# A hybrid transformer layer on one core: weights loaded behind the first stacks

## The reference

```
x = x + attn_a(layernorm(x))   # 32 heads of 8, window of 128 keys back, softmax, Wo
x = x + ffn(layernorm(x))      # 256 -> 1024 -> 256, relu, shared weights
x = x + attn_b(layernorm(x))   # rms norm, conv of 4 taps, delta-rule scan over time, gated MLP
x = x + ffn(layernorm(x))      # the same ffn again

def ffn(x1):
    w_up = ((q_up - 7.5) * repeat(s_up, 64, axis=1)).T          # q_* are int32 in 0..15
    y1 = x1 @ w_up + b_up + x1 @ w_up_lora_a @ w_up_lora_b       # rank 16
    x2 = relu(y1)
    w_down = ((q_dn - 7.5) * repeat(s_dn, 64, axis=1)).T
    return x2 @ w_down + b_down + x2 @ w_down_lora_a @ w_down_lora_b
```

## Time and profile before

| | us |
|---|---|
| median of 3 runs | 1243.53 (1241.19 to 1246.96) |
| the profiled execution | 1244.26 |
| its span in the profile | 1242.3 |
| busy: PE, PEld, DVE, ACT, POOL | 1037.7, 712.3, 917.8, 495.8, 179.0 |

### The profile page before, as it was taken

The page is one execution under the profiler, slowest core; times in us unless marked ns, Lnnn a source line. Parts: engine busy times, 40 slices in busy tenths (PEclk is TensorE's granted clock), DMA queues, the critical chain, the costliest instruction groups (busy, mean ns, idle before and its releaser), DMA issues.

```text
span 1242.3 us, 23054 instructions
## 1 busy us (share of the span) xinstructions
PE 1037.7 (84%) x9098; PEld 712.3 (57%) x9112; DVE 917.8 (74%) x2425; ACT 495.8 (40%) x1027; POOL 179.0 (14%) x267
## 2 busy tenths in 40 slices
PE   3589869967998999899988999899989978966467
PEld 2245635645556665666566755666566646744445
DVE  2733277898789778987898778977898678968911
ACT  2034254326443554326432644355443634541122
POOL 2200001040004000400040000300040004010400
PEclk9579879886999899989999999989998979997768
DMA  9813014302430133012410242014400200020000
GB/s 285 153 35 76 17 43 102 61 1 72 101 50 1 35 109 79 9 35 81 89 28 10 77 100 45 1 42 103 82 7 26 82 16 1 18 77 0 5 21 9
DMA packets 94123, 67.81 MB, mean 55 GB/s; under 512 B 47744, under 2 KB 86848, under 8 KB 94016
## 3 DMA queue, kind: packets, MB, share of 16 engines
q1 hardware_dynamic: 88544, 60.75, 20.9%
q10 hardware_dynamic: 4960, 5.54, 1.6%
q0 software_dynamic: 512, 0.05, 0.1%
HBM read 45.57 MB, written 20.32 MB: 53 GB/s over the span
## 4 chain that ended last, share of the span: by engine, by line
PE 47%; DVE 28%; ACT 9%; DMA 7%; SPq 4%; issue 3%; POOL 1%; ACTq 0%; DVEq 0%; POOLq 0%
PE bank L1612 6%; PE bank L1503 5%; PE bank L1757 5%; PE bank L1560 4%; PE bank L1684 4%; PE bank L1766 4%; PE bank L1592 4%; DMA q_l<-lane_q 4%; PE bank L1709 3%; DVE state L1235 3%; DVE lane_buf L1213 3%; PE bank L1555 3%; DVE state L1227 3%; DVE u_l L1222 2%; DVE mx L1023 2%
## 5 line engine op out<-in xcount | busy, mean ns | idle before, releaser
L715 ACT ACTIVATE probs<-bank 128x512 f32<-128x512 f32 x256 | 152.1, 597 | 187.4 <-PE bank L1597 187.3
L1612 PE MATMUL bank<-probs,v_ext 128*9 128x128 f32 x2048 | 164.9, 283 | 16.5 <-ACT probs L715 6.8
L1023 DVE TENSOR_REDUCE mx<-bank 128x2 f32<-128x320 f32 x256 | 120.9, 486 | 54.3 <-PE bank L1560 50.3
L341 POOL TENSOR_TENSOR lane_buf<-state,q_l 128x128 f32<-128x128 f32 x128 | 79.9, 654 | 339.7 <-DVEq L1242 339.7
L1757 PE MATMUL bank<-feat_c,wgu 128*128 128x256 f32 (+1 forms) x384 | 96.3, 402 | 23.6 <-DVE hid_c L1284 18.0
L1612 PEld LDWEIGHTS bank<-probs,v_ext 128*9 128x9 f32 x2048 | 91.3, 93 | 39.6 <-issue 18.0
L1592 PE MATMUL bank<-q_stack,k_stack 128*128 128x128 bf16 x1024 | 106.0, 229 | 2.7 <-DMA q_stack<-m_rows 2.7
L1555 PE MATMUL bank<-edge_mask,identb 128*128 128x128 bf16 x256 | 63.0, 246 | 52.6 <-DVE mx L1023 36.6
L1757 PEld LDWEIGHTS bank<-feat_c,wgu 128*128 128x128 f32 (+1 forms) x384 | 71.8, 192 | 44.1 <-DVE hid_c L1284 21.2
L1213 DVE TENSOR_TENSOR lane_buf<-state,til 128x128 f32<-128x128 f32 x256 | 84.5, 330 | 16.9 <-POOL lane_buf L602 10.2
L1560 PE MATMUL bank<-k_stack,q_stack 128*32 128x160 bf16 x2048 | 93.0, 265 | 0.0
(11 more groups left out here) (169 smaller groups left out, 1762.5 us busy)
## 6 DMA issues: line engine op xcount, KB each, us to landing
k_pieces<-conv SPq DMA_DIRECT2D x48, 128.0 KB, 2.3
k_stack<-k_pieces SPq DMA_DIRECT2D x32, 192.0 KB
k_stack<-k_pieces SPq DMA_DIRECT2D x32, 128.0 KB
k_l<-lane_k SPq DMA_DIRECT2D x8, 512.0 KB, 3.7
q_l<-lane_q SPq DMA_DIRECT2D x8, 512.0 KB, 5.7
q_pieces<-conv SPq DMA_DIRECT2D x24, 128.0 KB, 2.1
q_stack<-q_pieces SPq DMA_DIRECT2D x32, 96.0 KB
tok<-in_x SPq DMA_DIRECT2D x8, 256.0 KB, 3.2
```

What stands on the lines that cost most here:

```text
L715: act.activation(probs[:, u % 2], score_bank[u % 2][:], ACT.Exp, scale=float(DK) ** -0.5).then_inc(exp_done, 1)
L1023: dve.tensor_reduce(mx[:, g, 2 * v:2 * v + 2], bank[1 + u % 2][:].rearrange("p (h k) -> p h k", h=2)[:, :, 0:SPAN], AX.X, ALU.max).then_in ...
L1612: last = pe.matmul(bank[5][row:row + VE, col:col + W], v_ext[:, b, kb, h, :], probs[:, u % 2, (hp * 2 + kb) * W:(hp * 2 + kb + 1) * W], st ...
```

## The change

The launch, the data and what is computed stay the same. On each engine:

- SP: the nine weights, `wdown_b`, three constants (ones, head_sum, to_lanes, now part of `plain`), the residual's x and the quantised weights with their scales are issued behind the three first stacks and x of block 1. The low-rank factors, which ScalarE's queue had, come ahead of the pieces. Of the pieces SP writes the keys (`first_keys`).
- ScalarE issues two DMAs at the start instead of 12; computes rstd before the copies of the attention weights; issues the three DMAs of the query pieces; and copies the eight banks of low-rank products into `w_up` and `w_dn` (`lora_kept`). It waits for `weights_in` at the first relu of block 0 rather than ahead of the first maxima.
- VectorE clears `k_stack` first of all and sets up `k_stack` before `q_stack`. `up_weights` runs at the slot of step 20 (WEIGHTS_AT) of the first attention, its twin for `w_dn`, `down_weights`, and `delta_weights` behind `first_apply` of block 0. The dequantised values are written over the scales, then added to what ScalarE copied.
- GpSimd issues the six pad DMAs of the first three slots (`first_pads`), behind its 16 group rows.
- TensorE multiplies `ident` by `ident` 56 times (WARM) into a bank that the next turns overwrite; waits for `lora_kept` ahead of the maxima, and for weights where each is used first.

```diff
+WARM = 56
+WEIGHTS_AT = 20
...
@@ plain and consts
+            (ones[:], a["ones"]),
+            (head_sum[:], a["head_sum"]),
+            (to_lanes[:], a["to_lanes"]),
         ]
-        consts = [(ones[:], a["ones"]), (head_sum[:], a["head_sum"]),
-                  (to_lanes[:], a["to_lanes"]), (edge_mask_f, a["edge_mask"]),
-                  (tri_mask_f, a["tri_mask"]), (stack_cols[:], a["stack_cols"])]
+        consts = [(edge_mask_f, a["edge_mask"]), (tri_mask_f, a["tri_mask"]), (stack_cols[:], a["stack_cols"])]
...
@@ SP
+            def first_keys():
+                for p, cast in enumerate((piece1, piece2, piece3)):
+                    sp.wait_ge(cast, 2)
+                    for late in range(2):
+                        sp.dma_start(k_pieces[late, :, :, 2 - p, :, 1 - late].rearrange("h b p t -> p (h b) t"),
+                                     pieces[:, 1, p, :].rearrange("p (a t) -> p a t", t=W)).then_inc(pieces_out, 16)
+            def quantised():
+                sp.dma_start(q_up.rearrange("p (k n) -> p k n", k=KT),
                             a["q_up"].rearrange("(k p) n -> p k n", p=128)).then_inc(up_in, 16)
...
-            for dst, src in plain:
-                sp.dma_start(dst, src).then_inc(weights_in, 16)
-            for i, m in inner:
-                sp.dma_start(wdown_b[0:m, i, :], a["wdown_b"][128 * i:128 * i + m, :]).then_inc(weights_in, 16)
-            load_residual(0)
-            pieces_to_dram(0)
+            for dst, src in [(lora_a_up, a["lora_a_up"]), (lora_b_dn, a["lora_b_dn"]),
+                             (lora_b_up, a["lora_b_up"]), (lora_a_dn, a["lora_a_dn"])]:
+                sp.dma_start(dst, src).then_inc(lora_in, 16)
+            first_keys()
             sp.wait_ge(pieces_out, 144)
             sp.wait_ge(pad_out, 48)
             sp.wait_ge(stack_init, 2)
             for g in range(RING):
                 load_stacks(0, g)
-                load_pad(0, g)
-            sp.wait_ge(tok_next_ready, 1)
             load_x(1)
+            quantised()
+            load_residual(0)
+            for dst, src in plain:
+                sp.dma_start(dst, src).then_inc(weights_in, 16)
+            for i, m in inner:
+                sp.dma_start(wdown_b[0:m, i, :], a["wdown_b"][128 * i:128 * i + m, :]).then_inc(weights_in, 16)
@@ GpSimd
+            pool.wait_ge(stack_init, 2)
+            for r in range(RING):
+                load_pad(pool, 0, r, first_pads)
@@ ScalarE
             act.wait_ge(early_in, 16 * (len(early) + 2))
+            norm_next(0)
             for k in range(KT):
                 last = act.copy(wqkv_a[:, k, 0:2 * D].rearrange("p (a d h) -> p a d h", d=DK, h=HPH),
                                qk_staged[:, k].rearrange("p (a h d) -> p a d h", d=DK, h=HPH))
-            norm_next(0)
             turn_next(0)
...
+            act.wait_ge(piece3, 2)
+            for p in range(3):
+                act.dma_start(q_pieces[0, :, :, p].rearrange("h b p t -> p (h b) t"),
+                              pieces[:, 0, p, :].rearrange("p (a t) -> p a t", t=W)).then_inc(pieces_out, 16)
             values_out(0)
-            act.wait_ge(weights_in, 16 * (len(plain) + IT))
+            for k in range(KT):
+                for c in range(2):
+                    act.wait_ge(lora_prod, 2 * k + c + 1)
+                    act.copy(w_up[:, k, c * 512:(c + 1) * 512], bank[2 * k + c][:]).then_inc(lora_kept, 1)
+            for k in range(FT // 2):
+                act.wait_ge(lora_prod, 2 * KT + k + 1)
+                act.copy(w_dn[:, 2 * k:2 * k + 2, :].rearrange("p a n -> p (a n)"), bank[4 + k][:]).then_inc(lora_kept, 1)
@@ VectorE
+            def up_weights():
+                dve.wait_ge(up_in, 16 * (1 + 128 // QBLK))
+                dve.scalar_tensor_tensor(out=s_up, in0=q_up, scalar=-7.5, in1=s_up, op0=ALU.add, op1=ALU.mult
+                                         ).then_inc(scaled, 1)
+                dve.wait_ge(scaled, 1)
+                dve.wait_ge(lora_kept, 2 * KT)
+                w = w_up[:].rearrange("p k n -> p (k n)")
+                dve.tensor_tensor(w, w, s_up, ALU.add).then_inc(up_ready, 1)
+...
+            def delta_weights():
+                dve.wait_ge(weights_in, 16 * (len(plain) + IT))
+                for k in range(KT):
+                    for w, i in ((wqkv_b[:, k], 0), (wbeta[:, k], 0), (wout_b[:, k], 1), (wgu[:, k], 2)):
+                        last = dve.tensor_scalar(w, w, norm_w[:, i, k:k + 1], None, ALU.mult)
+                last.then_inc(weights_scaled, 1)
...
+            zero = mark(dve.memset(k_stack[:], 0.0))
+            norm_next_vars(0)
             dve.wait_ge(early_in, 16 * (len(early) + 2))
-            norm_next_vars(0)
@@ TensorE
+            for _ in range(WARM):
+                pe.matmul(bank[0][:, 0:128], ident[:], ident[:], start=True, stop=True)
             turn_next(0)
...
-            pe.wait_ge(lora_added, FT // 2)
-            pe.wait_ge(weights_scaled, 1)
+            pe.wait_ge(lora_kept, 2 * KT + FT // 2)
```

More of the change, by code:

```diff
@@ L348, in terms_of, with load_pad @@
             return last
+        def load_pad(queue, n, r, landed):
+            for e in range(CHUNK // (2 * W)):
+                queue.dma_start(k_stack[PADROW:PADROW + 1, r, :, 2 * W * e:2 * W * (e + 1)],
+                                a["pad_row"][:, n * W:(n + 2) * W].rearrange("a (o t) -> a o t", o=1)
+                                .broadcast_to([1, KC, 2 * W])).then_inc(landed, 16)
         def x2(n):
@@ L402, in load_stacks @@
                                  ).then_inc(stacks_in[r], 16)
-            def load_pad(n, r):
-                for e in range(CHUNK // (2 * W)):
-                    sp.dma_start(k_stack[PADROW:PADROW + 1, r, :, 2 * W * e:2 * W * (e + 1)],
-                                 a["pad_row"][:, n * W:(n + 2) * W].rearrange("a (o t) -> a o t", o=1)
-                                 .broadcast_to([1, KC, 2 * W])).then_inc(pad_in[r], 16)
             def next_stacks(n, g):
@@ L759, in relu_a @@
             def relu_a(n, i):
+                if n == 0 and i == 0:
+                    act.wait_ge(weights_in, 16 * (len(plain) + IT))
                 act.wait_ge(hid_done, n * FT + i + 1)
@@ L1344, in body @@
                     for at in range(4 * CUTS[0] if following else 0):
+                        if n == 0 and at == SLOT_AT[WEIGHTS_AT - BEGIN]:
+                            up_weights()
                         other = between(n, at, other, front)
@@ L1680, in ffn_up @@
             def ffn_up(n, i):
+                if n == 0 and i == 0:
+                    pe.wait_ge(up_ready, 1)
                 if i >= 2:
@@ L1869, in _ @@
                                  lora_a_dn[:, k * 128:(k + 1) * 128], lora_b_dn, start=True, stop=True)
-            last.then_inc(lora_prod, 1)
-            pe.wait_ge(lora_added, FT // 2)
-            pe.wait_ge(weights_scaled, 1)
+                if k % 2:
+                    last.then_inc(lora_prod, 1)
+            pe.wait_ge(lora_kept, 2 * KT + FT // 2)
             pe.wait_ge(consts_cast, 1)
```

89 lines of the change are left out of this document (45 added, 44 removed).

## The result

Over 20 runs of each, the changed kernel takes 1252.32 us in the median (1243.11 to 1260.53), the kernel before 1244.17 (1235.59 to 1250.76): a ratio of 1.0064 with a 95% interval of 1.0046 to 1.0082, so 8 us slower where 8 less were forecast. The profiled execution has a span of 1254.3 us. Its first residual add on VectorE comes at 139.90, against 131.58 before: 8.3 later, the difference of the medians. The rest of the span's 12 us lies behind it and is what one execution differs from another by; so this text compares medians, and places in the first 140 us.

What follows compares the result with a forecast made beforehand. Bound taken: the prologue, with SP's queue delaying the pieces some 12 us. Attention starting at 65.4 instead of 73.0 saves 7.6 us: profiled 1244.26 becomes 1236.7, median 1236; own range 1233 to 1240, whole range 1227 to 1243.

Steps and rivals of the forecast that it cites:

- First turn: Prologue: TensorE's first turn of x follows WARM's 15.9 us and comes at 21.4, 4.7 later than before.
- WARM is too long: Rival at the start: WARM's rows don't overlap and take 32 us, attention 8.8 later, 1252; chance 0.07.
- the clock stays up: Rival: TensorE's clock stays up through low-rank products and maxima; products end 4.2 sooner, 1230; chance 0.18.
- VectorE's moved work: Weight work moved to attention's step 20 and behind the first apply costs nothing; without cover, 4.5 and 8.3 us.
- Ahead of the fourth stack SP must be through with its weights, about 75 ... nothing, with some 4 us in hand: First attention: fourth stack issued at 76, needed at 88, drains in 6.4 us, so no wait.
- Bounds 0 and 3.5, I take 1.2: Before attention: SP's 8.8 MB load delays ScalarE's little DMAs of the maxima by 1.2 us.
- 65.4 forecast: Start of the first attention: 64.2 after the maxima plus 1.2 for the little DMAs, instead of 73.0.
- the 288 GB/s of 0 to 40 us: Rate assumed for SP's 8.8 MB behind the stacks, so that they load from 45 to about 76 us.
- The stack's drain of 6.4 us: Fourth stack: drain time taken from a stack issued alone at 83.63 and drained by 90.0.
- one row, 106.67: Evidence for pricing ScalarE's little DMAs: one took 4.87 us beside a stack's load, against 2.46 with idle queues.
- the late weights hold something up: Rival: late weights delay the maxima's rows or fourth stack, 3 to 6 us given back, 1240 or 1241; chance 0.22.
- ScalarE's DMA would lie near its lower bound: Maxima's rows: with queues served packet by packet, attention would start near the lower bound, 64.2.

Runs made afterwards that it cites:

- run 9: Changed kernel with the scales replaced by as many bytes of wgu, each DMA over 128 partitions instead of 64: 1237.38 us, 0.9938 of the kernel before.
- run 1: Changed kernel with the quantised weights and scales issued by SP ahead of the pieces: 1241.57 us, 0.9989 of the kernel before.
- run 5: Changed kernel with SP issuing the plain weights ahead of the quantised ones behind the stacks: 1245.54 us, 0.9988 of the kernel before.
- run 4: Changed kernel with the repeated scales replaced by as many bytes of distinct wgu rows, still over 64 partitions a DMA: 1253.11 us, 1.0075 of the kernel before.
- run 3: Changed kernel with SP holding the quantised weights and all behind them until the first attention's first scores: 1252.14 us, 1.0065 of the kernel before.
- run 2: Changed kernel with WARM set to 0 instead of 56: 1248.48 us, 1.0025 of the kernel before.
- run 8: Changed kernel with the fourth stack issued behind the quantised and ahead of the plain weights: 1252.21 us, 1.0045 of the kernel before.
- run 13: Changed kernel with the scales' upper 64 partitions issued by ScalarE, the lower half left to SP: 1246.96 us, 1.0013 of the kernel before.

## Why the prediction was wrong

*Right, to 60 us.* First turn 20.23 (forecast 21.4), end of the third casts 28.06 (29.6), first stack's DMA 32.90 (33.2), low-rank products from 30.89 (32.5), maxima from 42.72 behind a ScalarE copy (44.6), their turns from 60.49 (60.9). Part of the last agreement is luck: the maxima began 1.9 early, but TensorE waited 1.42 and 1.06 us for the second and third stacks, which the sum had put at nothing, so they took 17.8 instead of 16.3. The clock fell as forecast: 0.50 from 40 to 70. WARM took 14.84 against 15.9; "WARM is too long" and "the clock stays up" did not come.

*Right, behind attention.* VectorE's moved work costs nothing: the down-weights run at 143.58 and 145.90, and VectorE still sits idle for 9.90 us ahead of the second residual add, which follows the first by 22.7 as before.

*Wrong: the step "Ahead of the fourth stack SP must be through with its weights, about 75 ... nothing, with some 4 us in hand".* SP was through at 91.38 and the wait was 8.22. *And the term "Bounds 0 and 3.5, I take 1.2"* for the maxima's rows: from the first turn to attention it is 13.3 instead of 4.5, so 8.8 more. The account: 65.4 forecast, less 0.4 for the turn, plus 8.8, is the 73.8 measured; with the fourth stack's 8.2 that is 16.6 more than forecast. 1.5 come back at the fourth group's rows (a wait of 0.42 instead of 1.91), and 0.8 more are lost where no wait was traced. That makes 15.9, the first residual add's 139.90 against 124.0 by the forecast, and 1236 + 16 = 1252.

The first, the fourth stack's step, rested on one number, "the 288 GB/s of 0 to 40 us", carried over to another place. It was a mean over two kinds of load, and finer windows of the kernel before show them apart, the scales' stretch first:

```profile
16.00:20.00 4.00, 2.51 (x8) 1.90 (x9) 0.58 (x2) 0.58 (x1) 0.00 (x0) 1.00 1.16 245
20.00:24.00 4.00, 4.00 (x15) 3.15 (x13) 0.16 (x1) 0.58 (x1) 0.00 (x0) 1.00 1.15 237
...
28.00:32.00 4.00, 3.20 (x10) 1.53 (x10) 4.00 (x1) 0.65 (x2) 0.00 (x0) 1.00 1.07 394
```

But the mean is not what failed. By these rates 4.2 MB of quantised weights and scales at 240 and the other 4.6 MB at 394 take 29 us, by the mean 31. What failed is the carrying over: in its new place, behind the stacks' loads, the quantised part went at 139 to 169 GB/s, below anything in these windows, and SP stood in the whole load from 46 to 91 us, 45 us instead of 31. No window of the scales in the kernel before shows such a rate. The stack's drain of 6.4 us was carried over too, from a stack that was loaded alone; it took 12.3.

The second, the rows' bounds, went by one row, 106.67, that was 2.4 above the idle one; the upper bound of 3.5 has no row behind it. And that row lay beside engines that were not full:

```profile
105.00:110.00 5.00, 4.56 (x73) 2.68 (x67) 0.14 (x1) 3.09 (x6) 0.00 (x0) 1.00 0.69 102
```

Beside full engines the same DMA cost 3.7 to 4.1 more than the idle one's 2.46 even where the load was quick (6.18, 6.39 and 6.55 in runs 9, 1 and 5), and some 10 more in the changed kernel (issued at 61.12, landed by 73.75).

The forecast's rival "the late weights hold something up" named both places and gave them 3 to 6 us at a chance of 0.22. Its mechanism was right; 16.6 were lost. Run 9 is the check of the first term: with the load at 297 and 364 GB/s attention begins at 67.3, where the forecast had 65.4, and the fourth stack makes nobody wait. The 1.9 between are the rows' DMA, 6.18 beside a full load instead of 2.46 + 1.2, less 0.6 at the turns. That its median, 1237.4, comes so near to the forecast's 1236 is in part luck: its first residual add is 4.5 later than the forecast's 124.0.

What makes the load slow is shown as far as this: in this place it is the DMAs that write 64 partitions (run 4 against run 9). The Trainium skill has the rule that the prediction should have weighed (SBUF — State Buffer, section Door 1: The DMA port swizzle): a DMA to partitions 0 to 63 reaches 8 of 16 ports, and it gives 196 GB/s against 328 for 128 partitions. The slow stretches here, 139 to 174 against 273 to 382, agree in kind, and are lower than the page's 196. Three things stay open. The quantised values' own DMAs, over 128 partitions, were slow in the same queue (q_up took 15.4 us to land, 11.0 in run 9). With both halves written at once the rate stayed at 172; if half of the ports were all of it, it should have risen. And the same DMAs over 64 partitions were slow only in some runs: in the kernel before (from ScalarE's queue, mixed with plain weights from SP's) and in runs 1 and 3 (into an idle queue of SP's) the scales' windows show 192 to 245 GB/s; behind other loads in SP's queue (the changed kernel, runs 2, 5 and 8) they show 137 to 176. No run separates the queue's state from the rest, and 64 partitions alone do not explain the lower rate. The Trainium skill says too (DMA: Bandwidth & Descriptors, section Rules for kernel authors) that two halves serialize and that one transfer over 128 partitions should be used; run 13 agrees.

*The rule that the prediction did weigh* (the Trainium skill, DMA: Bandwidth & Descriptors, Queues, rings and completion order) is that DMA engines take turns between queues packet by packet. The prediction drew from it that ScalarE's DMA would lie near its lower bound. Here the 12 KB of the maxima's rows took 2.4 us on idle queues, 6.2 to 6.5 beside a quick load and 11.4 to 12.9 beside the slow one (runs 13 and 8). Taking turns may still be what happens, but it did not keep the DMA cheap.

## What to carry to other kernels

A load's rate belongs to its place and not to its bytes alone: the same quantised weights and scales went at some 240 GB/s in one place and at 165 in another, both at a full DMA share. So when a load is moved, give its rate a range of its own, and price every DMA beside it for full engines, not from a row beside half-busy ones. Look at the partitions and the outermost dimension of each DMA: here the same bytes over 128 partitions instead of 64 took the load from 165 to some 330 GB/s, and an outermost dimension of 2 left two engines. And when a queue's load is moved, follow every later item in that queue, not the first alone: here three different waits (rows, fourth stack, next block's pieces) took each other's place as the load was shifted.

## What had not been expected of the hardware

SP's issue of a DMA, mostly some 0.5 us, took 15.55 us for two (L447, from 49.51) in the middle of the slow load, and what stood behind it in SP's program started that much later. Six 4 KB pads, issued by GpSimd, took 1.7 us to land in the changed kernel, at a DMA share of 0.35 (20 to 30 us), and 5.9 in run 1 beside the load: GpSimd's small DMAs paid for it too. And the column of granted clock is no sign of TensorE's speed at the very start: it reads 1.00 from 0 to 30 us, but WARM's rows are 421 ns long up to about 10 us and 275 from there on, and without WARM the turn of x took 1.09 us instead of 0.60.
